# A two-layer graph convolution: root products and merge products move 96 columns instead of 128

## What is computed

```python
def _egnn_conv(x, src, dst, edge_attr, W_msg, W_edge, W_root, b):
    msg = x[src] @ W_msg + edge_attr @ W_edge
    agg = jax.ops.segment_max(msg, dst, num_segments=x.shape[0])
    agg = jnp.where(jnp.isneginf(agg), 0.0, agg)
    return agg + x @ W_root + b

c1 = leaky_relu(_egnn_conv(X,  src, dst, edge_attr, W1_msg, W1_edge, W1_root, b1))
c2 = leaky_relu(_egnn_conv(c1, src, dst, edge_attr, W2_msg, W2_edge, W2_root, b2))
out = layernorm(x + c2)
```

## Time and profile before

| | |
|---|---|
| median of three runs | 2085.36 us |
| the profiled execution | 2083.45 us |
| its span, first to last instruction | 2081.6 us |
| mean granted clock | 0.914 |
| TensorE matmul busy | 1620.9 us (78%) |
| TensorE weight load busy | 1408.5 us (68%) |
| VectorE, GpSimd, ScalarE busy | 1317.8, 1092.5, 1056.0 us |
| merge products (L556) | 4688 passes, 610.6 us busy |
| root products (L468) | 3136 passes, 460.3 us busy |

### The profile page before, as it was taken

One profiled execution on the slowest core, in us unless ns is written; L12 is line 12 of the kernel. 1 busy time (PEld: TensorE's weight loads), 2 busy tenths in 40 slices (PEclk: granted clock), 3 DMA queues, 4 the chain that ended last, 5 costly groups with the idle time before them and its releaser, 6 DMA issues.

```text
span 2081.6 us, 37108 instructions
## 1 busy us (share of the span) xinstructions
PE 1620.9 (78%) x11422; PEld 1408.5 (68%) x11422; DVE 1317.8 (63%) x2383; ACT 1056.0 (51%) x2450; POOL 1092.5 (52%) x1454
## 2 busy tenths in 40 slices
PE   3888888888888888886687888888888777666664
PEld 2657766667768888885566766676667666666664
DVE  2556666656666555553465655555654789999998
ACT  1323444334433455553344444443444678898897
POOL 6755666666640000002666666666664778766673
PEclk9988999999999999998899999889989989998887
DMA  6757888798874678885566766666767789999996
GB/s 122 187 132 217 232 240 230 214 243 229 231 222 176 203 237 261 271 279 188 142 183 181 196 189 185 191 188 177 197 182 233 221 268 294 306 301 291 297 293 195
DMA packets 580028, 459.13 MB, mean 221 GB/s; under 512 B 448559, under 2 KB 487346, under 8 KB 579842
## 3 DMA queue, kind: packets, MB, share of 16 engines
q1 hardware_dynamic: 497956, 301.88, 52.0%
q10 hardware_dynamic: 50910, 97.16, 12.6%
q0 software_dynamic: 30976, 57.72, 11.6%
HBM read 283.25 MB, written 173.37 MB: 219 GB/s over the span
## 4 chain that ended last, share of the span: by engine, by line
PE 52%; DVE 19%; another core or an unknown queue 10%; issue 10%; ACT 3%; POOL 3%; DMA 2%; ACTq 1%; SPq 1%; POOLq 0%; DVEq 0%
PE ps L556 17%; PE ps L468 14%; PE ps L459 8%; PE ps L437 6%; DVE stats L933 5%; PE ps L430 4%; DVE arena L931 3%; DVE arena L928 3%; PE ps L447 3%; POOL onehot L417 2%; DMA onehot_bytes<-arena 2%; DVE arena L951 1%; DVE arena L876 1%; ACT arena L620 1%
## 5 line engine op out<-in xcount | busy, mean ns | idle before, releaser
L556 PE MATMUL ps<-hold,onehot 128*128 x4688 | 610.6, 292 | 187.0 <-POOL onehot L417 136.9
L556 PEld LDWEIGHTS ps<-hold,onehot 128*128 128x128 f32 x4688 | 579.3, 204 | 218.4 <-issue 218.3
L384 POOL DMA_INDIRECT arena<-nodes,src_perm x392 | 370.8, 946 | 581.6 <-SPq L351 356.0
L468 PEld LDWEIGHTS ps<-w_root,onehot 97*128 97x128 f32 x3136 | 437.0, 209 | 170.0 <-issue 166.0
L468 PE MATMUL ps<-w_root,onehot 97*128 97x128 f32 x3136 | 460.3, 294 | 52.9 <-ACT arena L620 32.1
L384 POOL DMA_INDIRECT arena<-in_x_dram,src_all x392 | 377.7, 964 | 232.8 <-issue 115.0
L620 ACT COPY arena<-ps 128x384 f32<-128x384 f32 x392 | 188.2, 480 | 370.8 <-remote 241.3
L417 POOL CAST onehot<-keep 128x256 f32<-128x256 uint8 x588 | 302.2, 563 | 107.6 <-PE ps L556 64.5
L862 DVE TENSOR_TENSOR_SCAN arena<-keep,arena,ps 96x512 f32<-96x512 bf16 x196 | 248.3, 1267 | 142.1 <-remote 80.1
L459 PE MATMUL ps<-ident,arena 128*96 128x128 f32 x1568 | 262.3, 291 | 34.2 <-issue 27.7
L680 ACT COPY arena<-ps 128x384 f32<-128x384 f32 x392 | 166.7, 477 | 210.4 <-PE ps L556 210.4
(11 more groups left out here) (97 smaller groups left out, 1152.7 us busy)
## 6 DMA issues: line engine op xcount, KB each, us to landing
root<-arena ACTq DMA_DIRECT2D x196, 384.0 KB
arena<-root SPq DMA_DIRECT2D x196, 384.0 KB, 4.6
nodes<-arena SPq DMA_DIRECT2D x98, 384.0 KB, 2.8
arena<-nodes SPq DMA_DIRECT2D x98, 384.0 KB
arena<-in_x_dram SPq DMA_DIRECT2D x97, 384.0 KB
arena<-in_x_dram SPq DMA_DIRECT2D x48, 768.0 KB, 8.1
out_dram<-arena SPq DMA_DIRECT2D x48, 768.0 KB, 4.7
onehot_bytes<-arena ACTq DMA_DIRECT2D x147, 128.0 KB
```

What stands on the lines that cost most here:

```text
L384: nc.gpsimd.indirect_dma_start(out=gathered[t.ring][0:t.p, i, 0:D], out_offset=None, in_=table_in, in_offset=bass.IndirectOffsetOnAxis(ap= ...
L468: last = nc.tensor.matmul(no_ps[m % 2][:, i * P:(i + 1) * P], nodes_t[m % NODE_RING][0:D + 1, i * P:(i + 1) * P], w_root[0:D + 1, layer * ...
L556: nc.tensor.matmul(ps_bytes[:, bass.ds(place_at, SLOT)].bitcast(F32), onehot[:, k % NS, i, :], flat[:, bass.ds(chunk_at, P)], start=False, ...
```

## The change

In `root_of` the moving operand is exactly the 96 columns of this layer's weights, and the output is the first 96 columns of the slot. In `merge` the moving operand is the chunk's own 96 columns, and the output the first 96 columns (4 * D bytes) of the slot. The stationary operands, the places of slots, the padding and everything else stay as they are.

```diff
                 for i in range(C):
-                    last = nc.tensor.matmul(no_ps[m % 2][:, i * P:(i + 1) * P], nodes_t[m % NODE_RING][0:D + 1, i * P:(i + 1) * P],
-                                            w_root[0:D + 1, layer * D:layer * D + P], start=True, stop=True)
+                    last = nc.tensor.matmul(no_ps[m % 2][:, i * P:i * P + D], nodes_t[m % NODE_RING][0:D + 1, i * P:(i + 1) * P],
+                                            w_root[0:D + 1, layer * D:(layer + 1) * D], start=True, stop=True)
                 last.then_inc(no_full, 1)
...
-                        nc.tensor.matmul(ps_bytes[:, bass.ds(place_at, SLOT)].bitcast(F32), onehot[:, k % NS, i, :], flat[:, bass.ds(chunk_at, P)],
+                        nc.tensor.matmul(ps_bytes[:, bass.ds(place_at, 4 * D)].bitcast(F32), onehot[:, k % NS, i, :], flat[:, bass.ds(chunk_at, D)],
                                          start=False, stop=True, skip_group_check=True).then_inc(stepped[layer], 1)
```

## The result

The changed kernel takes 2104.08 us (median of 13 runs, 2089.81 to 2113.87) against 2085.32 us (13 runs, 2071.51 to 2098.72). The ratio is 1.0076, with a 95% interval of 1.0053 to 1.0099: it is slower, by about 16 us at this ratio. The prediction was 2078 us; the time lies inside its wide range (2044 to 2122), outside the forecast's own (2064 to 2094), and on the other side of no change.

A forecast was written before the change was run, and what follows sets the result against it. TensorE was taken to bound the first merge and pace the edge phases between DMA stalls. Terms of -3.5, -0.8, -7, -2, -2, +8 and +2 sum to -5.3 us: 2078 us, range 2044 to 2122 (forecast's own 2064 to 2094).

The forecast's parts named there:

- Cost of one pass, full clock: First merge and edge phases: weight load keeps passes 107 to 111 ns apart; -1.5 ns a pass, -3.5 and -2 us.
- Rivals A and C: First: passes fall to 82 ns, about 1970 us, chance 0.08; second: every small gain arrives, 2041 us, chance 0.10.
- Cost at the low clock: Edge phases and start of first merge: distance falls from 214 to 170 ns, -7 and -0.8 us.
- Second merge: Layer 1's merge: TensorE slows in more places, behind VectorE, DMA and GpSimd; +2 us (0 to +15).
- The clock: Edge phases: passes filled less with matmul bring stretches with waits nearer to a clock fall; +8 us (0 to +25).
- rival B: The clock falls, in the edge phases above all, then the first merge: +39 us, 2122 us; chance 0.20.
- What bounds the kernel: First merge: TensorE, matmuls busy 274 of 313 us; edge phases: TensorE between DMA stalls; second merge: room on TensorE.
- Ends of groups: Root copies in edge phases and GpSimd in second merge get a group's last product 28 ns sooner; -2 us.

The follow-up runs named there:

- e3: The changed kernel with both merges at 64 moving columns, sums of features 64 to 95 left out: 2349.45 us in one run.
- e4: The changed kernel with 96 of the 128 one-hot columns loaded in both merges, last 32 nodes of each block left out: 2093.87 us in one run.
- e1: The changed kernel with the merge of layer 1 back at 128 moving columns: 0.9997 of the time before the change.
- e2: The kernel before, with only the merge of layer 1 at 96 moving columns: 1.0076 of the time before.

## Why the prediction was wrong

**Cost of one pass, full clock: right.** The load keeps the distance: 112 ns stayed 112, well over the 105 that would have refuted it. The small gain that I took (-1.5 ns a pass, -5.5 us over the first merge and the edge phases) was nothing; the lower bound, 0, was the value. Rivals A and C fall with it. The evidence that I had was thinner than it looked: I read rows 8 as a second load that starts "before any product could hold it up", but the trace has the first product from 653.68 us, 0.01 us behind the first load. It took e3 and e4 to tell the load from the moving side. The Trainium skill ("TensorE: Matmul & The Clock Gate", LDWEIGHTS) puts a load at its stationary columns over 1.2 GHz, by an estimate from this rule 107 ns for 128. The distance of 112 ns at the full clock is near it; at the low one the runs show 213, and the measurement decides.

**Cost at the low clock: wrong.** I took 170 ns, from a load that I thought lengthened by half. It is 213: the load there takes twice its time as well (e3, e4), and eight root passes take 1.65 us in the chain after, not the 1.3 to 1.4 that I named. My 170 ns put a gain of 7.8 us into the sum that was not there, and, worse, hid the loss.

**Second merge: the step that failed.** I gave it +2 us (0 to +15) behind a cover of 143 us of idle time. It measured +23 us, and +17 between e1 and e2. Idle time in total is not a cover: what counts is whether a batch at the low clock takes longer than the stretch has for one. With my 170 ns it was 2.7 us against 3.2, and there was room; with 214, which rows 9 had, it is 3.4 and there is none. I also priced a fall of the clock in the edge phases alone, although this was the stretch in which TensorE waited most; here it fell from 0.90 to 0.80. What it is about a narrower pass that lets the clock fall for longer, the runs don't show.

**The clock: mechanism right, place wrong.** I put +8 us, and rival B's +25, into the edge phases. Their clock stayed at 0.91 and 0.92 in the profile after. In e1's runs they lost some, about 57 us more at the low clock; at my 0.23 that would be +13 us, and the measured change is -5 to +4. So the price was wrong there as well. The first merge kept its clock. B had the sign, but its "point from which it decides" named two stretches that lost no time.

**What bounds the kernel.** I called the first merge TensorE's own, and meant its passes. It is TensorE's issue as much: passes shortened from 112 to 90 ns on average left it at 326 us (e4, one run). By that run, even a full success in the pass would have brought nothing there.

**Ends of groups.** The size was right, the reason wrong: I read it off a shorter record, near 247 ns. Only a group's first root product has one (248 ns), the others stay at 275, but all behind the first start sooner after their loads, so a root group does end 26 ns sooner. As time this can't be told from nothing (e1).

## What to carry to other kernels

Ask which side of a product sets the distance between passes before cutting the other: with a fresh fp32 load of 128 columns for each product, moving columns under 128 saved no time here. Then price TensorE at the low clock in every stretch where it waits, by the time that one unit of work takes there against the time that the stretch has for it; a stretch bound by another engine can change hands with no wait added. Padding that looks like waste can be what holds the clock, as the 32 columns of the second merge did here (0.90 with them, 0.80 without).

## What the runs showed of the hardware that I had not expected

- The load of the stationary operand of an fp32 product holds passes apart at both clocks: 112 and 213 ns for 128 columns; for 96, 160 at the low one. After a rest at the low clock the second load starts only 0.17 us after the first (643.73 and 643.89 us in the trace before), and this is not the distance in a stream.
- A pass starts while the record of its load still runs: 109 ns after the load's start with 128 moving columns and 82 with 96, where the load's record lasts 192.
- With 64 moving columns behind loads of 128, the clock stayed at 0.50 through 500 us of products without a pause and through a merge of 550 us with products for 513 (e3). Busy passes alone did not bring the full clock back.
- Reading register values from memory on TensorE's queue takes 0.6, 1.1 and 2.3 us at the median for 8, 16 and 32 words.
